# Two attentions and two mixtures of experts on one core: statistics, passage order, gather buffers, and rounds written out

## What is computed

```python
# x: (64, 64, 256)   ctx_1024: (64, 64, 128)   all float32
x = x + tanh(g_xattn[0]) * xattn0(layernorm(x), ctx)   # 32 heads of 8, axial rotation of q and k, softmax, Wout + bout
x = x + tanh(g_ffn[0])   * ffn0(layernorm(x))          # shared expert (704, silu gate, sigmoid gate) + 8 experts of 176, top 2 by softmax
x = x + tanh(g_xattn[1]) * xattn1(layernorm(x), ctx)   # 16 heads of 128 over 8 key/value heads, mask, softmax, Wo
x = x + tanh(g_ffn[1])   * ffn1(layernorm(x))          # router tanh(x Wg1) Wg2, top 2; silu(x Wup + bup) Wdown + bdown, 8 x 128 hidden
```

## Time and profile before

| | |
|---|---|
| median of three runs | 1691.07 us (1688.68 to 1693.64) |
| profiled execution | 1688.36 us |
| its span in the trace | 1686.6 us |
| mean granted TensorE clock | 0.971 of full |
| instructions in the trace | 41092 |

### The profile page before, as it was taken

The page is one execution under the profiler, slowest core; times in us unless marked ns, Lnnn a source line. Parts: engine busy times, 40 slices in busy tenths (PEclk is TensorE's granted clock), DMA queues, the critical chain, the costliest instruction groups (busy, mean ns, idle before and its releaser), DMA issues.

```text
span 1686.6 us, 41092 instructions
## 1 busy us (share of the span) xinstructions
PE 1524.0 (90%) x14338; PEld 1293.2 (77%) x14338; DVE 1158.1 (69%) x2994; ACT 751.4 (45%) x1529; POOL 564.3 (33%) x682
## 2 busy tenths in 40 slices
PE   3899999997998889999969999999999999988986
PEld 2566666665777778999869988999889998977875
DVE  5888888887666666545546777777777777656866
ACT  2466666663223322555524444444444444434632
POOL 3555655550323331000011123333222223134556
PEclk8899999999999999999979999999999999998999
DMA  7566666571101001543320011111111111014635
GB/s 197 120 129 129 129 128 123 118 143 36 51 29 48 26 26 48 163 143 126 132 76 26 26 36 35 37 38 34 34 34 34 35 34 34 23 57 139 200 118 163
DMA packets 148997, 137.24 MB, mean 81 GB/s; under 512 B 12986, under 2 KB 138611, under 8 KB 148508
## 3 DMA queue, kind: packets, MB, share of 16 engines
q1 hardware_dynamic: 138076, 106.38, 25.3%
q0 software_dynamic: 10816, 29.54, 5.5%
HBM read 64.69 MB, written 71.19 MB: 81 GB/s over the span
## 4 chain that ended last, share of the span: by engine, by line
PE 64%; DVE 19%; issue 6%; ACT 4%; SPq 3%; DMA 2%; POOL 1%; ACTq 0%; DVEq 0%; POOLq 0%
PE bank L647 12%; PE bank L648 11%; PE bank L649 11%; PE bank L1158 5%; PE bank L709 3%; PE bank L1192 3%; PE bank L718 2%; PE bank L732 2%; PE bank L673 2%; PE bank L749 2%; PE bank L1172 1%; PE bank L736 1%; ACT pT_a L1400 1%; POOL yg_f L1951 1%; PE bank L695 1%
## 5 line engine op out<-in xcount | busy, mean ns | idle before, releaser
L1904 POOL TENSOR_TENSOR probs_b<-probs_b,rs_b 128x512 f32<-128x512 f32 x64 | 66.9, 1046 | 300.8 <-DVE rs_b L2769 298.8
L647 PE MATMUL bank<-xT_b_hi,m_hi 128*128 128x256 f32 x512 | 151.3, 296 | 7.0 <-ACT xT_b_hi L1605 5.0
L1885 POOL DMA_INDIRECT xn_b<-sorted_y,place_of x62 | 59.8, 965 | 291.0 <-DMA sorted_y<-ys 180.2
L647 PE MATMUL bank<-n_hi,oT_b_hi 128*128 128x256 f32 x512 | 148.9, 291 | 3.5 <-DVE x L2596 2.5
L648 PE MATMUL bank<-xT_b_hi,m_lo 128*128 128x256 f32 x512 | 145.8, 285 | 0.0
L649 PE MATMUL bank<-xT_b_lo,m_hi 128*128 128x256 f32 x512 | 145.6, 284 | 0.0
L649 PE MATMUL bank<-n_lo,oT_b_hi 128*128 128x256 f32 x512 | 145.0, 283 | 0.0
L648 PE MATMUL bank<-n_hi,oT_b_lo 128*128 128x256 f32 x512 | 144.8, 283 | 0.0
L1420 ACT ACTIVATE probs_a<-probs_a 128x512 f32<-128x512 f32 x128 | 80.4, 628 | 114.2 <-DVE probs_a L2076 113.8
L1610 ACT ACTIVATE qT<-bank 128x512 f32<-128x512 f32 x128 | 75.1, 597 | 122.9 <-PE bank L649 62.0
L1158 PEld LDWEIGHTS bank<-ctxT_b,qT 128*128 128x128 f32 x1024 | 125.1, 193 | 2.7
(11 more groups left out here) (410 smaller groups left out, 4764.9 us busy)
## 6 DMA issues: line engine op xcount, KB each, us to landing
sorted_x<-zeros SPq DMA_DIRECT2D x16, 2112.0 KB, 14.0
xg<-sorted_x SPq DMA_DIRECT2D x71, 128.0 KB, 2.1
sorted_y<-ys SPq DMA_DIRECT2D x71, 128.0 KB, 2.0
xg<-sorted_x SPq DMA_DIRECT2D x31, 256.0 KB, 2.9
sorted_y<-ys SPq DMA_DIRECT2D x31, 256.0 KB, 2.6
w_raw<-in_w SPq DMA_DIRECT2D x16, 408.0 KB, 3.9
x<-in_x SPq DMA_DIRECT2D x4, 1024.0 KB, 7.2
cx_raw<-in_ctx SPq DMA_DIRECT2D x32, 128.0 KB, 2.7
```

The lines of the kernel that those rows point to most:

```text
L647: pe.matmul(dst, lh, rh, start=start, stop=False, skip_group_check=True)
L1885: pool.indirect_dma_start(out=rows[:, c, :], out_offset=None, in_=ys_dram, in_offset=bass.IndirectOffsetOnAxis(ap=place_of[:, c, tile:tile ...
L1904: pool.tensor_tensor(probs_b[b], probs_b[b], rs_b[:, b, :].unsqueeze(2).broadcast_to([P, G1, S]), ALU.mult).then_inc(s["b_probs"], 1)
```

## The change

- First feed-forward: `stats_g` is split into `moments_g` (bn_stats, bn_aggr) and `stats_g` (the Newton chain). For block i + 2 they stand in slots 2 and 3 of block i, and `norm_g(i + 2)` in slot 6, so `xn` gets a third buffer and the semaphores `rows_moved` go by i % 3. Only `norm_g(1)` stays in slot 0 of block 0.
- First attention: the statistics of tiles 0 to 7 go from the last round into round 14, on VectorE alone, in four pieces (`late`), and VectorE's loop ends a round earlier.
- Passage: ScalarE takes the root of round 0's statistics behind `n_hi[4]`; `shift_of_b` and `norm1(0)` move to c == 5; the gather of tile 3 goes to `yg1`; tiles 2 and 3 are added and round 1's statistics and `norm1(1)` made before round 0; in round 0 the parts of round 1's turned rows come earlier.
- Last stage: five gather buffers, and the adds by a table `ADDS` of block and slot.
- Second attention on TensorE and ScalarE: `rounds_b` gives way to all 16 rounds written out.
- Semaphores `m_psum`/`n_psum`, `m_copied`/`n_copied` and `sel_cleared`/`bd_cleared` are merged in pairs.

The diff, cut to its core:

```diff
-SLOTS = {"f0": dict(norm=0, t0=1, t1=2, logits=3, back=4, largest=4, weigh=5, place=7),
+SLOTS = {"f0": dict(norm=0, t0=1, t1=2, logits=3, back=4, largest=4, weigh=5, place=7, moments=2, stats=3, ahead=6),
...
-NX1, NH1, NY1, NG1, NB1 = 4, 3, 3, 3, 4
+NX1, NH1, NY1, NG1, NB1 = 4, 3, 3, 5, 4
...
+GATHERED = ("y_gathered", "y_gathered1", "y_gathered2", "y_gathered3", "y_gathered4")
+ADDS = {(0, 4): (0,), (0, 5): (1, 2), (0, 6): (3,), (0, 7): (4, 5), (0, 8): (6, 7), (0, 9): (8,),
+        (1, 0): (9, 10), (1, 1): (11,), (1, 2): (12, 13), (1, 3): (14, 15), (1, 4): (16,), (1, 5): (17, 18), (1, 6): (19,),
+        (1, 7): (20, 21), (1, 8): (22,), (1, 9): (23,)}
...
+        f0["xn"].append(r.take("f0_xn2", FT, D))
...
+        def shared_rows(n):
+            return 16 * TOP * FT * len(range(n, NF, 3))
+
...
-                    m = pe.transpose(turned(i)[:, t * P:(t + 1) * P], f0["xn"][i % 2][:, t, k * P:(k + 1) * P], ident)
+                    m = pe.transpose(turned(i)[:, t * P:(t + 1) * P], f0["xn"][i % 3][:, t, k * P:(k + 1) * P], ident)
...
-            pe.wait_ge(s["n_copied"], H1 // 2)
+            pe.wait_ge(s["mn_copied"], H1)
...
-            rounds_b(pe, attend1)
+            attend1(0, first=True)
+            attend1(1)
+            for i in range(2, NR + 2):
+                attend1(i, route=i % 2)
+            attend1(NA - 2, late=True)
+            attend1(NA - 1, last=True)
...
             for c in range(H1 // 2):
-                act.wait_ge(s["m_psum"], c + 1)
+                act.wait_ge(s["mn_psum"], c + 1)
                 act.activation(m_hi[:, 2 * c:2 * c + 2].rearrange("p u k c -> p (u k c)"), bank[c % 4][:, :], ACT.Copy).then_inc(
                     s["scalar_steps"], 1)
             for c in range(H1 // 2):
-                act.wait_ge(s["n_psum"], c + 1)
+                act.wait_ge(s["mn_psum"], H1 // 2 + c + 1)
                 act.activation(n_hi[:, 2 * c:2 * c + 2, :].rearrange("p u n -> p (u n)"), bank[4 + c % 4][:, :],
                                ACT.Copy).then_inc(s["scalar_steps"], 1)
+                if c == 4:
+                    act.wait_ge(s["stats_ready"], 2)
+                    act.activation(sd[:, 0:4], sd[:, 0:4], ACT.Sqrt).then_inc(s["scalar_steps"], 1)
             NB = 4
...
                     act.activation(dl1, dl1, ACT.Tanh, scale=0.5).then_inc(s["g_exp_ready"], 1)
                 expo(1)
+                if first:
+                    xT_high1(i + 1)
                 act.wait_ge(s["b_cx_loaded"], i * 32 + 32)
                 act.wait_ge(s["b_o_psum"], START + i * 8)
...
                     xh_f(i)
                 expo(2)
-                if not last:
+                if not first and not last:
                     xT_high1(i + 1)
                 if route is not None:
...
-                                                in_=f0["xn"][i % 2][:, t, :], in_offset=None).then_inc(s[f"rows_moved{i % 2}"], 16)
+                                                in_=f0["xn"][i % 3][:, t, :], in_offset=None).then_inc(s[f"rows_moved{i % 3}"], 16)
...
                         pool.wait_ge(s[f"x_stored{n}"], 16 * len(range(n, NJ, NY)))
                 else:
-                    if tile != 1:
+                    if tile == 3:
+                        pool.wait_ge(s["c_added"], 2)
+                    elif tile != 1:
                         pool.wait_ge(s["c_added"], tile)
                     if tile % 2 == 0:
                         pool.wait_ge(s["b_xnT_psum"], START + tile // 2)
-                rows = yg1 if tile == 1 else yg
+                rows = yg1 if tile in (1, 3) else yg
                 for c in range(TOP):
                     pool.indirect_dma_start(out=rows[:, c, :], out_offset=None, in_=ys_dram,
...
                     pool.memset(f1["bd_raw"], 0.0).then_inc(s["bd_cleared"], 1)
-                    pool.memset(f1["sel"].bitcast(F32), 0.0).then_inc(s["sel_cleared"], 1)
+                    pool.memset(f1["sel"].bitcast(F32), 0.0).then_inc(s["bd_cleared"], 1)
                 if j == 5:
-                    pool.wait_ge(s["sel_cleared"], 1)
+                    pool.wait_ge(s["bd_cleared"], 2)
                     pool.dma_start(f1["sel"][0:KC].rearrange("p c m -> p (c m)"), a["sel1"]).then_inc(s["sel1_cast"], 16)
...
                     pool.wait_ge(s["c_added"], NT + tile - NG1 + 1)
-                done = s[("y_gathered", "y_gathered1", "y_gathered2")[n]]
+                done = s[GATHERED[n]]
                 for c in range(TOP):
...
-            def stats_g(i, count=FT):
-
-                for t in range(count):
+            def moments_g(i):
+
+                for t in range(FT):
                     st.done(ve.bn_stats(bn[:, t, :], x[:, i * FT + t, :]))
                 st.wait()
-                for t in range(count):
+                for t in range(FT):
                     st.done(ve.bn_aggr(mv_new[:, t, :], bn[:, t, :]))
                 st.wait()
-                rsqrt(rstd[:, i * FT:i * FT + count], nmr[:, i * FT:i * FT + count], 8, count)
+
+            def stats_g(i):
+                rsqrt(rstd[:, i * FT:i * FT + FT], nmr[:, i * FT:i * FT + FT], 8, FT)
...
             def norm_g(i):
-                if i >= 2:
-                    ve.wait_ge(s["g_xT_psum"], (i - 1) * KT)
-                    ve.wait_ge(s[f"rows_moved{i % 2}"], 16 * TOP * FT * (i // 2))
+                if i == 2:
+                    ve.wait_ge(s["rows_cleared"], 16 * NA)
+                if i >= 3:
+                    ve.wait_ge(s["g_xT_psum"], (i - 2) * KT)
+                    ve.wait_ge(s[f"rows_moved{i % 3}"], 16 * TOP * FT * (i // 3))
                 for t in range(FT):
-                    st.done(normalise(f0["xn"][i % 2][:, t:t + 1, :], i * FT + t))
+                    st.done(normalise(f0["xn"][i % 3][:, t:t + 1, :], i * FT + t))
                 st.wait()
...
                         resid0(i - 1, 1)
-                    if p == 0 and last:
-                        stats_g(0, 2 * FT)
+                    if late and p < 2:
+                        for t in range(FT):
+                            st.done(ve.bn_stats(bn[:, FT * p + t, :], x[:, FT * p + t, :]))
+                    if late and p == 2:
+                        st.wait()
+                        for t in range(2 * FT):
+                            st.done(ve.bn_aggr(mv_new[:, t, :], bn[:, t, :]))
+                    if late and p == 3:
+                        st.wait()
+                        rsqrt(rstd[:, 0:2 * FT], nmr[:, 0:2 * FT], 8, 2 * FT)
                     if p == 1 and last:
...
             ve.wait_ge(s["tables_rest"], 64)
-            with ve.Fori(1, NA - 1) as i:
+            with ve.Fori(1, NA - 2) as i:
                 st.loop(i, STEPS["a"], 1)
                 attend0(i)
-            st.end(NA - 1)
+            st.end(NA - 2)
+            attend0(NA - 2, late=True)
             attend0(NA - 1, last=True)
...
                             weights_low(i + 1, 1 - u)
-                    if i == 0 and t >= 1:
-                        add_f(t - 1)
-                    if i == 1:
-                        add_f(9 + t + t // 2)
-                        if t % 2 == 1:
-                            add_f(10 + t + t // 2)
+                    for tile in ADDS.get((i, t), ()):
+                        add_f(tile)
                 ve.wait_ge(s[f"{ph}_down_done"], START + i * chunks + chunks)
...
                     if i + 1 < NF:
-                        if t == at["norm"]:
-                            norm_g(i + 1)
+                        if i == 0 and t == at["norm"]:
+                            norm_g(1)
                         if t == at["t0"]:
...
                             slots_g(i + 1)
-                            if i + 2 < NF:
-                                stats_g(i + 2)
                     else:
...
                             places_g()
+                    if i + 2 < NF:
+                        if t == at["moments"]:
+                            moments_g(i + 2)
+                        if t == at["stats"]:
+                            stats_g(i + 2)
+                        if t == at["ahead"]:
+                            norm_g(i + 2)
                 resid_g(i)
...
-            def shift_of_b(i):
-                ve.wait_ge(s["scalar_steps"], H1 + i + 1)
+            def shift_of_b(steps):
+                ve.wait_ge(s["scalar_steps"], steps)
                 st.done(ve.reciprocal(rr_b, sd[:, 0:4]))
...
                 ve.tensor_tensor(m_lo[:, 2 * c:2 * c + 2].rearrange("p u k c -> p (u k c)"), bank[c % 4][:, :],
-                                 m_hi[:, 2 * c:2 * c + 2].rearrange("p u k c -> p (u k c)"), ALU.subtract).then_inc(s["m_copied"], 1)
+                                 m_hi[:, 2 * c:2 * c + 2].rearrange("p u k c -> p (u k c)"), ALU.subtract).then_inc(s["mn_copied"], 1)
             for c in range(H1 // 2):
-                ve.wait_ge(s["scalar_steps"], H1 // 2 + c + 1)
+                ve.wait_ge(s["scalar_steps"], H1 // 2 + c + (2 if c > 4 else 1))
```

(72 more changed lines are left out.)

## The result

The changed kernel takes 1652.47 us at the median of four runs (1650.61 to 1653.05), the kernel before 1691.39 (four runs, 1688.68 to 1693.64): a ratio of 0.9769, 95% interval 0.9752 to 0.9786, so 38.9 us faster. The forecast was 1651.6. The profiled execution took 1653.05 us with a span of 1651.1, which is 35.4 us under the span of before.

What follows compares the result with a forecast made beforehand. TensorE, busy 90% of the span, bounds the kernel through its waits and half-clock stretches. Gains 20.7 + 4.7 + 10.3 + 3.8 = 39.5 us give 1648.9 us profiled, 1651.6 at the median; range 1640 to 1674.

Steps and rivals of the forecast that it cites:

- likeliest case: Whole kernel: the forecast sum of 39.5 us holds, 1651.6 us at the median; chance 0.58.
- Part 2: End of first attention: statistics moved into round 14 cut TensorE's wait and half clock; gain 4.7 us, bounds 1.8 and 5.7.
- part 5: Second attention's rounds written out, semaphores merged: value 0, since the loop's back edge costs nothing beyond an ordinary border.
- Part 1: First feed-forward: moved statistics and normalisation remove 14.9 us of turn_g waits and 5.8 of slow clock; gain 20.7, lower bound 10.6.
- a sign of being wrong: First feed-forward: a new VectorE wait of over 0.5 us per block would show the prediction wrong.
- lower bound of 1.8: End of first attention: least gain, 8.5 - 6.7 = 1.8 us, if none of VectorE's idle time is used.
- Part 3: Passage and round 0 of second attention: queries 3.6 us earlier, first score to outputs1(0,0) 19.1 us; gain 10.3, bounds 5 and 13.
- Part 4: Last stage: five buffers and lagging adds free GpSimd's gathers, 5.5 - 1.7 = 3.8 us gained; bounds 1 and 5.5.
- ends of 0 and 6: Second attention's written-out rounds: bounds on their gain, 0 and 6 us, the upper from the first rival.
- rival (a): Second attention: written-out rounds gain 12 x 0.5 = 6 us more if registers behind loop waits cost; 1645.6 us, chance 0.10.
- Rival (b): Whole kernel: VectorE does not hide the moved work, lower bounds hold together, 18.4 us gained, 1672.7 us; chance 0.22.
- Rival (c): Second attention: code for written-out rounds comes late, 34 exposed packets cost 71 us, 1723 us, slower; chance 0.06.

Runs made afterwards that it cites:

- only_tail: The kernel before with only the statistics of tiles 0 to 7 moved into round 14 of the first attention, semaphores merged: 0.9979 of the kernel before.
- spread: Changed kernel with later adds, early high part, and statistics of tiles 0 to 7 spread over first-attention rounds 12 to 14: 1631.32 us, 0.9636 of the kernel before.

## Why the prediction was right, and where it was not

The forecast of 39.5 us met 38.9, and its likeliest case is the one that came: the waits that it named went, and most of the gain is where it put it. That the total came within 0.6 us is luck in part. Part 2 was put some 3 us too high and part 5 some 3 us too low, for reasons that have nothing to do with each other; and on the profiled pair, for which the sum was made, the gain is 35.4, after 2.4 lost in a stage that nothing touched.

- **Part 1**, 20.7 forecast, 21.5 in the runs and 19.1 in the profiled pair. `turn_g` waits once for the normalised rows, 1.12 us, and the clock is 1.00 from the first `place_g` to the last, as said. Four full blocks last 29.7 us each and the last two 31.2, since a wait of 1.3 us is new in each: the prediction had named a new VectorE wait of over 0.5 us as a sign of being wrong, and in two blocks it came. VectorE's `f_hl`, just ahead of `f_xT_lo`, takes 2.47 us in place of 0.68 while GpSimd splits weights and scatters. The step that took the whole 3.6 and 3.7 us of these two blocks as gained was 2.6 too high. That the runs give more than the pair fits the slow stretches that the one profile of before did not have and that of `only_tail` had; their interval holds both values.
- **Part 2**, 4.7 forecast, 0.3 between the five and the six profiles, 1.9 where block 0 stays at full clock, 1.2 in the runs without and with it, 3.6 alone (0.3 to 6.6). This is the step that failed; in five of seven profiles it fell under its lower bound of 1.8. Two terms of it were wrong. What comes back of the 6.66 was put at 3.8: it is 4.9, since idle time fell by 1.8 us alone. The prediction set the sum of a round's idle time, 1.21 and 2.67, against the pieces, but the 3.3 us of Newton steps stand at p = 3 with only the 1.2 near them, and 3.07 came back as a wait; round 14 itself is 1.7 us longer and not 4. And the 1.8 of half clock was taken as gone with the long wait: the wait of 3.07 has a slow stretch of its own behind it, and in five of the seven block 0 has another. `spread` puts the same work into the 2.67 and saves 6.7 in its one profile.
- **Part 3**, 10.3 forecast, 9.5 in the profiled pair, 10.8 alone. The queries begin 21.3 us after the first m product in place of 25.4, so 4.1 sooner (3.6 forecast). `outputs1(0,0)` comes 19.8 us after the first score (19.1 forecast) and waits 1.12 us, in which its `add_tile(4)` waits 0.60 for the gather, the wait that the prediction named; the half clock ahead of it is there too. In four other profiles of this order the stretch took 17.5 to 18.3 us with a wait of 2.5 at its end, and in one 21.8, mostly at half clock: here too the clock's part changes from one profile to the next.
- **Part 4**, 3.8 forecast, 3.6 and 3.9. VectorE still holds the gathers 2.9 us in 7 times, in place of 7.9 in 8. Beyond the ordinary 0.3 each that is 0.8, where the count of the new order gave 1.7, and the gathers take 62.5 us from first to last in place of 67.4, 4.9 less and more than forecast. The end came only 3.6 sooner because the gathers no longer set it: VectorE's last operation on x now waits for TensorE, 1.20 us, where before it followed the last add at once. So the total of this part is right with two errors in it. VectorE at the end of the changed kernel:

```profile
1646.32 1.41 DVE L2323 SCALAR_TENSOR_TENSOR x<-bank,gates,x 128x512 f32<-128x512 f32 x2 [1.20 <-PE bank L657]
```

GpSimd's waits of the changed kernel from 1570 us on:

```profile
POOL yg_f L1976 <- issue: 12.2, 40, 0.3
...
POOL yg_f L1976 <- DVE x L2936: 2.9, 7, 0.9
```

- **Part 5**, 0 forecast, 3.2 measured, inside its ends of 0 and 6. The mechanism is that of rival (a) at half its size. The argument against it, that this matmul waits for work and not for an instruction, is half of the truth: it does wait for `ptl(0)`, but the prediction did not look at how long after the end of `ptl(0)` it starts, 0.33 us in round 4. The written-out round 1 of the kernel before was the place to compare it with: its `ptl(0)` ends at 930.05, and the matmul starts 0.10 us later. What the prediction said of the back edge holds: two rounds on either side of one last the same, and the cost is at every real wait and not at the edge. The rule of the Trainium skill (Runtime: NRT & Kernel Launch, Instruction fetch mechanics) points to the edge; no run here shows a cost there.
- Rival (b), moved work that VectorE does not hide, is true of part 2, and on a small scale of the last two blocks of part 1 and of the wait for `add_tile(4)` in part 3. Rival (c) fell: 30 more instruction packets, 34 at most forecast, and the written-out rounds are shorter than the loop's, so no wait for code shows in them.

## What to carry to other kernels

Idle time of an engine is usable only where it lies: before work is moved into a round, name the instruction ahead of which the gap stands, and put there a piece no longer than the gap. Where TensorE waits with the releaser called issue, look at what the other engines finished just before, and at how long after it the matmul starts; against a written-out copy of the same round that tells the cost of a loop. And a change of 0.2% is to be read from windows of the rounds it touches, since slow stretches elsewhere hide it in the whole. The first attention's loop on TensorE stands in every kernel of this study; what it costs was not tried.

## What was not expected of the hardware

A wait of TensorE inside its hardware loop is answered 0.30 to 0.38 us after the releasing instruction ends, the same wait written out 0.10 us after. And the same blocks with waits of 1.9 us and more at their borders took between 215.5 and 222.9 us from one profile to the next (five kernels, one execution of each), with mean clocks of 0.97 and 0.95; without these waits 196.5 to 196.6 in nine profiles. There the waits cost more than their length, and by an amount that changed from profile to profile.
